# Turned rows a chunk further ahead of the scan, and a partition's four rows side by side in DRAM

## What is computed

```python
def _sage_conv(x, src, dst, Wl, bl, Wr):
    msg = x[src]
    summed = segment_sum(msg, dst, num_segments=N_NODES)
    cnt = segment_sum(ones, dst, num_segments=N_NODES)
    mean = summed / maximum(cnt, 1.0)[:, None]
    return mean @ Wl.T + bl + x @ Wr.T
h = relu(_sage_conv(x, src, dst, Wl0, bl0, Wr0))
h = relu(_sage_conv(h, src, dst, Wl1, bl1, Wr1))
h = _sage_conv(h, src, dst, Wl2, bl2, Wr2)
x = _layernorm(x + h)
# second layer: edge attention with softmax per source node
x = _layernorm(x + _L1_gnn_ref(x, edge_attr, ...))
```

## Time and profile before

| | us |
|---|---|
| median of 3 runs | 2632.78 (2631.59 to 2633.68) |
| profiled execution | 2643.03 |
| its span | 2641.2 |
| busy in it: PE, DVE, ACT, POOL | 1787.9, 1719.1, 1142.2, 1778.3 |

### The profile page before, as it was taken

The page is one execution under the profiler, slowest core; times in us unless marked ns, Lnnn a source line. Parts: engine busy times, 40 slices in busy tenths (PEclk is TensorE's granted clock), DMA queues, the critical chain, the costliest instruction groups (busy, mean ns, idle before and its releaser), DMA issues.

```text
span 2641.2 us, 42521 instructions
## 1 busy us (share of the span) xinstructions
PE 1787.9 (68%) x9906; PEld 1270.0 (48%) x9906; DVE 1719.1 (65%) x5656; ACT 1142.2 (43%) x2655; POOL 1778.3 (67%) x1895
## 2 busy tenths in 40 slices
PE   4755667988879889676777663888788788770000
PEld 2335665656656656455555453555555555540000
DVE  7777886878767778565555533888788788871000
ACT  7951112545445545132222222776666666640000
POOL 0047775676657666467777777777777777776776
PEclk7558989999999999788888885999999999985555
DMA  0025666899989998544444613455545445433321
GB/s 20 1 65 145 166 158 137 187 175 187 182 173 184 202 176 182 152 139 122 129 134 133 171 59 106 145 158 155 145 139 151 144 147 153 148 95 106 93 92 51
DMA packets 366865, 357.05 MB, mean 135 GB/s; under 512 B 46547, under 2 KB 288862, under 8 KB 366722
## 3 DMA queue, kind: packets, MB, share of 16 engines
q1 hardware_dynamic: 310274, 246.46, 30.9%
q0 software_dynamic: 56448, 109.10, 22.9%
HBM read 232.89 MB, written 129.11 MB: 137 GB/s over the span
## 4 chain that ended last, share of the span: by engine, by line
POOL 23%; issue 21%; DVE 20%; PE 15%; DMA 9%; ACT 8%; DVEq 1%; SPq 1%; POOLq 1%; ACTq 0%
POOL hsrc L672 9%; POOL GX L672 8%; POOL out_dram L726 4%; DVE stats L1347 4%; PE bank L849 4%; DMA GX<-in_x_dram,idx_a 2%; PE bank L923 2%; PE bank L771 2%; PE bank L853 2%; ACT normed L1017 2%; DVE prod L1392 2%; DMA XN<-in_x_dram 2%; ACT hsrc L1062 2%; ACT normed L1018 2%; DVE res L1339 2%
## 5 line engine op out<-in xcount | busy, mean ns | idle before, releaser
L672 POOL DMA_INDIRECT GX<-mean_product,idx_a x392 | 416.2, 1062 | 125.4 <-issue 113.8
L672 POOL DMA_INDIRECT GX<-in_x_dram,idx_a x392 | 378.9, 967 | 117.8 <-issue 109.1
L849 PE MATMUL bank<-h,wt 128*128 128x512 f32 x588 | 328.2, 670 | 1.2 <-ACT h L1036 0.9
L1047 ACT ACTIVATE logv<-mv,eps 128x4 f32<-128x4 f32 x245 | 72.3, 295 | 518.7 <-DVE mv L1352 518.6
L726 POOL DMA_INDIRECT x_prime<-normed,idx_b x196 | 198.5, 1013 | 88.0 <-issue 81.7
L726 POOL DMA_INDIRECT out_dram<-XN,idx_b x196 | 193.1, 985 | 74.7 <-issue 63.4
L672 POOL DMA_INDIRECT hsrc<-x_prime,idx_d x196 | 190.3, 971 | 59.7 <-issue 59.7
L672 POOL DMA_INDIRECT GX<-in_edge_attr_dram,idx_a x196 | 189.3, 966 | 58.6 <-issue 54.1
L672 POOL DMA_INDIRECT hsrc<-x_prime,idx_c x196 | 186.3, 951 | 59.7 <-issue 59.7
L1385 DVE TENSOR_TENSOR_SCAN seg<-flag,seg,hsrc 128x512 f32<-128x512 bf16 x98 | 126.1, 1286 | 115.5 <-ACT hsrc L1062 73.4
L869 PEld LDWEIGHTS bank<-wt,h 128*128 128x128 f32 x1176 | 153.0, 194 | 49.8 <-issue 47.4
(11 more groups left out here) (222 smaller groups left out, 4584.2 us busy)
## 6 DMA issues: line engine op xcount, KB each, us to landing
mean_product<-prod SPq DMA_DIRECT2D x147, 256.0 KB, 4.0
hsrc<-mean_product SPq DMA_DIRECT2D x147, 256.0 KB, 4.3
XN<-in_x_dram SPq DMA_DIRECT2D x98, 256.0 KB, 6.4
x_prime<-normed SPq DMA_DIRECT2D x98, 256.0 KB
XN<-x_prime SPq DMA_DIRECT2D x98, 256.0 KB, 4.5
out_dram<-normed SPq DMA_DIRECT2D x98, 256.0 KB
flag<-same_dst_row SPq DMA_DIRECT2D x147, 128.0 KB, 5.5
XN<-low_row SPq DMA_DIRECT2D x98, 128.0 KB
```

Source lines behind the costliest of these rows:

```text
L672: pool.indirect_dma_start(buf[:, c.slot(U), t, :], None, table, bass.IndirectOffsetOnAxis(ap=idx[:, c.slot(U), t:t + 1], axis=0)).then_inc ...
L849: last = pe.matmul(psum[:, :], wt[:, T_R[i], :], before[:, c.slot(2), :], start=True, stop=not dst_phase)
L1047: act.activation(logv[:, s, :], mv[:, s, :, 1], ACT.Ln, bias=eps[:, 0:1]).then_inc(n_log.of(c), 1)
```

## The change

Two edits. In mean1 and mean2 `mean_turn` on PE and `mean_keep` on ACT have lead 4 in place of 3; DVE's `mean_seg` stays at 3. And `sorted_rows` puts the rows 4 q to 4 q + 3 of a chunk into partition q, as `file_rows` does. The order in which the rows stand in SBUF and the running order of the scan stay as they are, so a sorted place t * 128 + q now has its row at 4 q + t of the chunk in the table. `make_table` therefore swaps the bit fields of its places: bits 7 and 8 (t) go to 0 and 1, bits 0 to 6 (q) go to 2 to 8, and the chunk's bits stay. The attended rows are stored and loaded with the same arrangement, and need no such step.

```diff
         def sorted_rows(table, c):
-            return take(table, c.index() * CH, CH).rearrange("(t q) d -> q t d", q=P)
+            return take(table, c.index() * CH, CH).rearrange("(q t) d -> q t d", t=TPC)
...
-                    run(pe, f"mean{i}", [(1, mean_prod), (3, mean_turn), (DENSE + 4, dense(chain_t)), (DENSE + 3, dense(chain_1)),
+                    run(pe, f"mean{i}", [(1, mean_prod), (4, mean_turn), (DENSE + 4, dense(chain_t)), (DENSE + 3, dense(chain_1)),
...
-                    run(act, f"mean{i}", [(3, mean_keep), (DENSE + 4, dense(keep_t)), (DENSE + 3, dense(keep_1)),
+                    run(act, f"mean{i}", [(4, mean_keep), (DENSE + 4, dense(keep_t)), (DENSE + 3, dense(keep_1)),
...
-                    part_i = marks_c[:, a, :].bitcast(I32)
+                    part_i, tile_i, four_i = marks_c[:, a, :].bitcast(I32), marks_g[:, a, :].bitcast(I32), marks_w[:, a, 0:COLS].bitcast(I32)
+                    link(dve.tensor_scalar(tile_i, marks_t[:, a, :], 7, TPC - 1, ALU.logical_shift_right, ALU.bitwise_and))
+                    link(dve.tensor_scalar(four_i, marks_t[:, a, :], P - 1, 2, ALU.bitwise_and, ALU.logical_shift_left))
+                    link(dve.tensor_scalar(part_i, marks_t[:, a, :], 9, 9, ALU.logical_shift_right, ALU.logical_shift_left))
+                    link(dve.tensor_tensor(tile_i, tile_i, four_i, ALU.bitwise_or))
+                    link(dve.tensor_tensor(marks_t[:, a, :], part_i, tile_i, ALU.bitwise_or))
```

## The result

The changed kernel takes **2649.6 us** in the median of 20 runs, before 2633.9 us in 20 runs beside it; the ratio is **1.0056, 95% interval 1.0043 to 1.0069**. So it is 0.56% slower, clear of the noise, where 2611 us had been predicted, with a range of 2575 to 2640 us. The profiled execution has a span of 2647.6 us (2641.2 before).

A forecast was written before the change was run, and what follows sets the result against it. A loop through DVE and ACT was taken as the bound, DMA engines just behind. 25 us less in mean1 and mean2 and 3.4 us more for the table of places made -21.6 us: 2611 us, range 2575 to 2640.

The follow-up runs named there:

- e3: Kernel before, with nodes without incoming edges looking up 128 different rows of zeros in place of one: ratio 0.9882, 2609.7 us.
- e5: Kernel before, with the lead of 4 and 128 rows of zeros, without the new arrangement of rows (512 B pieces): ratio 0.9671, 2555.3 us.
- e10: Kernel before, with every lookup of mean1 and mean2 sent to the one row of zeros, neighbours' means left out: ratio 1.0992, 2923.5 us.
- e6: The whole change, with 4 different rows of zeros, 2 KB apart, in place of one: ratio 0.9654, 2553.1 us.
- e4: The whole change, with 128 different rows of zeros looked up in place of one: ratio 0.9673, 2554.0 us.

## What to carry to other kernels

A high share of the DMA engines isn't yet work for them. Divide it by the packets of each kind, and where the same transfer costs nearly three times as much in one stage as in another, look at the addresses before counting bytes. Padding that sends many lookups to one row is such an address. Spreading it gave 1.2% here by itself (e3), and only with it was the better pipeline worth something, 2.1% more (e5); without it, the better pipeline lost. When a loop between engines is opened, ask what else has been running at nearly its rate.

## What the runs showed of the hardware

One 512 B row of DRAM, asked for by every gather, was read 65 to 70 times per us (33 to 36 GB/s) while the gathers of e10 ran beside other transfers, with the sixteen DMA engines taken for 97 to 98%. Over whole passes, pauses included, it was 51 to 56 times per us in three kernels. For 6 us with next to no other transfer more was seen. Queues of the kernel before, 764 to 770 us:

```profile
q0 software_dynamic: 185, 0.40, 92.5%
q1 hardware_dynamic: 52, 0.04, 3.3%
```

About 92 packets of 8 rows in 6 us, with 65.2% of them the one row: some 80 per us, an estimate, with the sixteen engines taken for 96%. Spread over four rows 2 KB apart or over 128, the limit wasn't met: the gathers took 17.2% of the engines over 480 to 1040 us, in e6 and in e4. 2 KB pieces moved at 365 GB/s, scaled to full engines, and 512 B pieces at 297. Over whole passes the hardware queue took 2.90 us per MB after and 3.07 before, and that made no difference to the time of any kernel here that can be told from noise.
